# One of a block's three picked tiles is made inside the softmax, in spare columns of the sums' bank, and a block's first group has no pick

## The chip, the cores and the metric

The kernel runs on one core of one Trainium2 chip. The metric is device time in microseconds (us) of one execution. The engines named below are PE (TensorE, matrix multiply), DVE (VectorE), ACT (ScalarE), POOL (GpSimd) and SP (SyncE, which here only waits, loads registers and issues DMAs).

## The reference, cut to what matters

Four graph layers run one after another on a graph of N = 3125 nodes and E = 100000 edges, sorted by destination. The change touches only the second one, a GATv2 network with three attention layers. Each computes, for every edge, a logit from two node rows, a softmax over the edges that end in the same node, and a weighted sum:

```python
for Wl, bl, Wr, br, att, bo, g, be in layers:      # three layers
    h_new = gelu(layer_norm(gatv2(h, src, dst, n, Wl, bl, Wr, br, att, bo), g, be))
    h = h + h_new if h.shape == h_new.shape else h_new

def _gatv2(h, src, dst, n, Wl, bl, Wr, br, att, bias):
    xl = (h @ Wl + bl).reshape(n, H, C)            # 4 heads of 32
    xr = (h @ Wr + br).reshape(n, H, C)
    e = leaky_relu(xl[dst] + xr[src], 0.2)
    logit = einsum('ehc,hc->eh', e, att)
    ex = exp(logit - segment_max(logit, dst)[dst])
    alpha = ex / (segment_sum(ex, dst)[dst] + 1e-16)
    return segment_sum(alpha[..., None] * xr[src], dst).reshape(n, H * C) + bias
```

## The kernel before

`attention` (L614 on) is called three times. Edges are cut into 800 tiles of 125; four tiles are a *quad*, so there are 200 quads. Destination nodes are cut into 25 windows of 125. A *step* is a quad with one window that it touches: 224 steps. Sixteen steps are a *block* (14 blocks, numbered from 0), four steps a *group* (4 groups in a block, i = 0 to 3).

**Source rows.** A tile needs 125 rows of `xr`, picked by `src`. Most come by POOL, one indirect DMA a tile (L565), into a ring of 20 quads (`rows`). The fourth tile of every fifth quad (40 tiles in all, the *picks*) is made by PE instead: DVE writes a one-hot matrix `hot_n` of 3125 x 125 in three cuts of windows (`point`, L941 to L946, each a compare of the tile's source numbers, laid out in PSUM as `wide_srcs`, against the node numbers), PE multiplies it with `xr` in 25 matmuls, again in three cuts (`pick`, L860 to L866), into `mixture`, columns of the second bank of `turn`; ACT copies it out and stores it to memory (`store_picked`, L750 to L756), and SP fetches it into the ring when its quad comes up (`fetch`). Thus POOL issues 760 indirect DMAs an attention. Four picks are made ahead; then blocks 0 to 11 make three each, in their groups 0, 1 and 2; blocks 12 and 13 make none.

**Who lets POOL go on.** POOL works down the quads in order (`gather_quads`). Before quad x it waits on `kept` (L563), which SP raises (`free`, in `pass_quads`) when quad x - 20 has been weighed by DVE for the last time (`weighted`). SP also passes on to PE, by `here` (L590), that a quad has landed.

**A block's steps.** For step k of block b, PE spreads the destination rows and adds the source rows (`spread_rows`, L835 to L847, matmuls L843 and L846, one step ahead of DVE), DVE makes the logits (`logits`, L977, L981, L984). In the same turn DVE weighs the rows of step k - 16, the same step of the block before (`weigh`, L992), PE sums them (`sum_rows`, L857), and DVE adds the sums on (`add_team`, L1000). So rows stay in the ring from their logit until the block's softmax is done and a block later they are weighed. Block 0 weighs nothing (`alone` in DVE's code, `spreads` in PE's and ACT's).

**The softmax between two blocks.** PE transposes the logits (L873). DVE runs eight scans (L1010, L1011); PE transposes their ends (L877) and then the carries (L881); DVE shifts the logits by the maxima (L1032 to L1038); ACT exponentiates them (L760); PE loads the next four steps' numbers into registers (`step_places`) and transposes the weights back (L887) and makes one small matmul (L888); ACT makes `fade` (L762); DVE copies the weights to `tail` and fades the running sums (L1042 to L1051). Then the next block begins: ACT lays out the source numbers of its picks (`lay`, L748, it waits for the softmax's end, since these lie in the bank that the softmax uses), and DVE's first instruction is the first `point`, which waits for it.

The order of every engine's work is the order of the code; semaphores alone tie the engines together.

Of the kernel before, what the change touches and what calls it, by code (L numbers as in the profile page):

```python
# [15 lines left out]
E = 100000  # L16
# [37 lines left out]
LAST = (PICKS - FIRST) // PER  # L54
assert RING % PICK == 0 and FIRST <= GROUP and PER <= GROUP and E // RROWS == 2 * HALF * P and FIRST + PER * LAST == PICKS and LAST < BLOCKS - 1
GROUPS = (WIN + 3) // 4
# [364 lines left out]
def hold(eng, sem, value, held_up):  # L421


    eng.wait_ge(sem, value)
    eng.sem_inc(held_up, 1)
# [222 lines left out]
def attention(nc, g, table, xl, xr, ft, att, own_att, own_logit):  # L648
# [4 lines left out]
    with Scope(nc) as sc:  # L653
# [39 lines left out]
        held_up_too = sc.sem("held_up_too")  # L693
        srcs_in, laid, noded, mixed, evicted, stored, fetching, returned = (sc.sem(x) for x in ("srcs_in", "laid", "noded", "mixed", "evicted", "stored", "fetching", "returned"))
# [28 lines left out]
        def _(act):  # L723
# [25 lines left out]

            def store_picked(t):  # L750
# [3 lines left out]
                act.copy(picked, mixture).then_inc(evicted, 1)  # L754
# [25 lines left out]

            with act.Fori(0, PER) as i:
                spreads(i)
                store_picked(i + FIRST)
            if PER < GROUP:
                with act.Fori(PER, GROUP) as i:
                    spreads(i)
            for q in range(2):
                load_hot(q, q)
            weigh(0)

# [6 lines left out]

            def block_of(b, per):
                if per:
                    with act.Fori(0, per) as i:  # L800
                        group(b, i)
                        store_picked(PER * b + i + FIRST)
                if per < GROUP:
                    with act.Fori(per, GROUP) as i:
                        group(b, i)
                weigh(b)

            with act.Fori(1, LAST) as b:
                lay(b + 1)
                act.wait_ge(laid, b + 2)  # L810
                load_srcs(PER * b + PER + FIRST)
                block_of(b, PER)
            with act.Fori(LAST, BLOCKS) as b:
                block_of(b, 0)
            last = TEAMS - BSTEPS
# [15 lines left out]
        def _(pe):  # L831
# [27 lines left out]

            def pick(t, r):  # L860
                pe.wait_ge(noded, len(CUTS) * t + r + 1)
                if r == 0 and not (isinstance(t, int) and t == 0):
                    pe.wait_ge(evicted, t)
                for w in range(*CUTS[r]):
                    ins = pe.matmul(mixture, hot_n[:, w, :], xr[:, w, :], start=w == 0, stop=w == WIN - 1)  # L865
# [24 lines left out]

            def four_steps(b, i, places=None, picking=True):
                for q in range(AHEAD):
                    k = BSTEPS * b + AHEAD * i + q
                    if q or not (isinstance(i, int) and i == 0):
                        sum_rows(k - BSTEPS - 1, (q - 1) % AHEAD)
                    if places is None:
                        places = step_places(nc, pe, g, k + 1)
                    if picking and q:
                        pick(PER * b + i + FIRST, q - 1)
                    spread_rows(k + 1, GROUP * b + i + (q + 1) // AHEAD, (q + 1) % AHEAD, places[q])  # L900
# [7 lines left out]
            def spreads(i, picking):  # L908
                places = step_places(nc, pe, g, AHEAD * i + 1)
                for q in range(AHEAD):  # L910
                    if picking and q:
                        pick(i + FIRST, q - 1)
                    spread_rows(AHEAD * i + q + 1, i + (q + 1) // AHEAD, (q + 1) % AHEAD, places[q])

            with pe.Fori(0, PER) as i:
                spreads(i, True)
            if PER < GROUP:
                with pe.Fori(PER, GROUP) as i:
                    spreads(i, False)
            def block_of(b, per, picked_by):  # L920
                four_steps(b, 0, softmax(b - 1, picked_by=picked_by), per > 0)
                if per > 1:
                    with pe.Fori(1, per) as i:
                        four_steps(b, i)
                if per < GROUP:
                    with pe.Fori(max(per, 1), GROUP) as i:
                        four_steps(b, i, None, False)
                sum_rows(BSTEPS * b - 1, AHEAD - 1)

            with pe.Fori(1, LAST) as b:  # L930
                block_of(b, PER, PER * b + FIRST)
            with pe.Fori(LAST, BLOCKS) as b:
                block_of(b, 0, PICKS)
            softmax(BLOCKS - 1, more=False)
# [5 lines left out]
        def _(dve):  # L940
# [45 lines left out]
            def choose(b, i, q):  # L986
                if q < len(CUTS):
                    point(PER * b + i + FIRST, i, q)

# [64 lines left out]

            dve.wait_ge(laid, 2)

            def alone(i, picking):
# [5 lines left out]

            with dve.Fori(0, PER) as i:
                alone(i, True)
            if PER < GROUP:
                with dve.Fori(PER, GROUP) as i:
                    alone(i, False)
            softmax(0)
# [15 lines left out]

            def block_of(b, per):
                both(b, 0, per > 0)
                if per > 1:
                    with dve.Fori(1, per) as i:
                        both(b, i, True)  # L1090
                if per < GROUP:
                    with dve.Fori(max(per, 1), GROUP) as i:
                        both(b, i, False)
                ws = windows_of(nc, dve, g, BSTEPS * b - 2, 2)
# [4 lines left out]
            with dve.Fori(1, LAST) as b:  # L1099
                dve.wait_ge(laid, b + 2)  # L1100
                block_of(b, PER)
            with dve.Fori(LAST, BLOCKS) as b:
                block_of(b, 0)
            last = TEAMS - BSTEPS
# [1628 lines left out]
```

## Time and profile before

| | us |
|---|---|
| median of 3 runs | 6526.3 (6516.55 to 6531.65) |
| profiled execution, its own time | 6522.1 |
| profiled execution, span of its trace | 6520.3 |

Busy time is 4622.5 us on PE (71% of the span), 3864.3 us on DVE (59%), 3852.1 us on POOL (59%), 1597.9 us on ACT (25%). The three attentions take from about 1080 to 2300 us, 2388 to 3600 us and 3694 to 4920 us of the span. A timeline row reads: start in us, duration in us, engine, line, operation, output<-input, and in brackets the idle time before it with what ended it. "issue" means that nothing which the profile shows was waited for; an engine's name with q is its sequencer, so `SPq L577` is SP's raising of `kept`.

### The profile page before, as it was taken

Reading aid. Unit: us, or ns where it says so; the run is one execution under the profiler, and the core shown is the slowest. Engines: PE = TensorE matmul, PEld = TensorE weight load, DVE = VectorE, ACT = ScalarE, POOL = GpSimd, SP = SyncE. Lnnn points to the kernel's source line nnn. Section 1 sums busy time; section 2 is a strip of 40 time slices with the busy share of each in tenths; the row PEclk is TensorE's granted clock in tenths of the full one; section 3 lists DMA queues with packets and bytes.
Section 4 is the critical chain, followed back from the end, with each engine's and each line's share of the span. In section 5 each row is a group of like instructions: output and inputs, shape, how many; then the busy total and the mean of one; then the engine's idle time right before and its main releaser. Section 6 shows DMA issues by size and latency. Waiting matters only on the chain. (4 is left out here: it accounts for less than half of the span.)

```text
span 6520.3 us, 133948 instructions
## 1 busy us (share of the span) xinstructions
PE 4622.5 (71%) x34231; PEld 4074.0 (62%) x34232; DVE 3864.3 (59%) x9164; ACT 1597.9 (25%) x3365; POOL 3852.1 (59%) x3152
## 2 busy tenths in 40 slices
PE   7868874787888747888887477887763656666665
PEld 5765334677777646777776467777762455555554
DVE  8988126666666566666665766666656433333334
ACT  4764110111111111111111111111111144444443
POOL 0000002778787726887877268878780078888884
PEclk9989986898888878988887788888886778778777
DMA  6863441333333323333333233333331122222221
GB/s 160 221 167 117 121 121 49 80 98 98 98 99 97 96 68 80 98 99 99 99 96 96 68 79 98 99 98 97 93 99 43 47 66 66 65 65 65 66 65 46
DMA packets 633590, 600.24 MB, mean 92 GB/s; under 512 B 244880, under 2 KB 571807, under 8 KB 632685
## 3 DMA queue, kind: packets, MB, share of 16 engines
q0 software_dynamic: 250880, 233.27, 15.7%
q10 hardware_dynamic: 229475, 208.97, 11.0%
q1 hardware_dynamic: 153097, 156.30, 9.0%
q8 instruction: 71, 1.16, 0.1%
q14 instruction: 67, 0.54, 0.0%
HBM read 497.47 MB, written 97.37 MB: 91 GB/s over the span
## 5 line engine op out<-in xcount | busy, mean ns | idle before, releaser
L565 POOL DMA_INDIRECT rows<-row_table,now x2280 | 2829.2, 1241 | 1640.8 <-issue 1527.6
L565 POOL DMA_INDIRECT rows<-node_table,now x800 | 989.9, 1237 | 562.9 <-issue 562.9
L977 DVE SCALAR_TENSOR_TENSOR z<-zp,own 125x512 f32<-125x512 f32 x672 | 464.1, 691 | 832.7 <-PE zp L846 828.1
L857 PEld LDWEIGHTS sums<-both,hot 125*125 125x125 f32 x5376 | 773.9, 201 | 186.9 <-issue 125.8
L857 PE MATMUL sums<-both,hot 125*125 125x137 f32 x5376 | 808.7, 297 | 101.6 <-ACT both L739 73.9
L846 PE MATMUL zp<-rows,ident 125*125 x2700 | 819.2, 430 | 70.2 <-SPq L590 68.9
L865 PE MATMUL turn<-xr,ft 125*125 125x132 f32 x6000 | 785.9, 289 | 70.2 <-DVE ft L946 66.1
L843 PE MATMUL zp<-parts,hot_t 125*125 x8100 | 654.7, 234 | 242.3 <-issue 183.6
L865 PEld LDWEIGHTS turn<-xr,ft 125*125 125x125 f32 x6000 | 760.1, 200 | 76.6 <-DVE ft L946 68.9
L843 PEld LDWEIGHTS zp<-parts,hot_t 125*125 125x125 bf16 x8100 | 614.1, 145 | 278.7 <-issue 276.5
L738 ACT CAST hot<-hot 125x500 f32<-125x500 bf16 x672 | 408.7, 608 | 1479.9 <-PE sums L857 751.1
L846 PEld LDWEIGHTS zp<-rows,ident 125*125 125x125 f32 x2700 | 492.1, 203 | 135.6 <-issue 77.6
L1273 DVE TENSOR_TENSOR z<-zp,rows 125x512 f32<-125x512 f32 x224 | 155.0, 692 | 628.8 <-SPq L590 503.5
L1206 PE MATMUL turn<-ident,onehot 125*126 125x125 f32 x904 | 175.6, 328 | 484.6 <-issue 464.7
L992 DVE TENSOR_TENSOR both<-rows,xl 125x512 f32 (+1 forms) x672 | 462.3, 688 | 87.7 <-PE sums L857 81.6
L946 DVE TENSOR_TENSOR ft<-turn,nodes 125x1125 f32<-125x1125 f32 x360 | 447.4, 1244 | 95.7 <-ACT turn L748 46.3
L981 DVE TENSOR_REDUCE both<-z 125x16 f32<-125x512 f32 x672 | 456.6, 679 | 1.6
L1206 PEld LDWEIGHTS turn<-ident,onehot 125*126 125x126 f32 x904 | 115.5, 165 | 529.2 <-issue 507.0
L1223 PE MATMUL sums<-values,onehot 125*125 125x129 f32 x1792 | 331.4, 346 | 0.0
L1214 PE MATMUL zp<-pb,onehot_t 126*125 x1792 | 327.7, 343 | 2.8 <-issue 0.6
L1498 DVE TENSOR_SCALAR hot<-nodes,both 125x522 bf16<-125x522 f16 x896 | 315.6, 416 | 19.1 <-PE bank L1537 18.8
L1214 PEld LDWEIGHTS zp<-pb,onehot_t 126*125 126x125 f32 x1792 | 306.8, 257 | 10.6 <-issue 8.2
(454 smaller groups left out, 5575.7 us busy)
## 6 DMA issues: line engine op xcount, KB each, us to landing
hot<-hots ACTq DMA_DIRECT2D x896, 122.1 KB
hot_t<-hots_t ACTq DMA_DIRECT2D x678, 122.1 KB
counts<-pairs SPq DMA_DIRECT2D x55, 685.1 KB
rows<-row_table,now POOLq DMA_INDIRECT x2280, 3.6
spread_slots<-slot_table POOLq DMA_DIRECT2D x56, 488.3 KB, 5.5
hots_t<-hot_t SPq DMA_DIRECT2D x112, 218.8 KB
hots<-hot_dst SPq DMA_DIRECT2D x112, 218.8 KB
pairs<-cells SPq DMA_DIRECT2D x25, 685.1 KB
```

The source lines that it names most:

```text
L565: pool.indirect_dma_start(rows[:, q, j, :], None, table, bass.IndirectOffsetOnAxis(ap=now[:, n, lane + j:lane + j + 1], axis=0)).then_inc( ...
L738: act.copy(hot32[:, q % 2, :], hot[:, q, :]).then_inc(made, 1)
L843: pe.matmul(zp[:, p, j, 0:ROW], hot_t[:, q, j * P:(j + 1) * P], own[part], start=part == 0 and j % 2 == 0, stop=False, skip_group_check=True)
L846: ins = pe.matmul(zp[:, p, 2 * half:2 * half + 2, 0:ROW], g.ident[0:P, 0:P], rows[:, bass.ds(at, 1), 2 * half:2 * half + 2, :].rearrange(" ...
L857: ins = pe.matmul(sums[:, p, 0:ACCW], hot32[:, p, j * P:(j + 1) * P], values[:, p, j, :], start=j == 0, stop=j == HALF - 1)
L865: ins = pe.matmul(mixture, hot_n[:, w, :], xr[:, w, :], start=w == 0, stop=w == WIN - 1)
L946: dve.tensor_tensor(hot_n[:, lo:hi, :], src, each(nodes[:, lo:hi], P), ALU.is_equal).then_inc(noded, 1)
L977: dve.scalar_tensor_tensor(out=z[:, p, :, :], in0=zp[:, p, :, 0:D], scalar=0.0, in1=rows_of(own_att, HALF), op0=ALU.max, op1=ALU.mult).the ...
L981: dve.tensor_reduce(bent[:, p, :, :], z[:, p, :, :].rearrange("p j (h c) -> p j h c", h=HEADS), AX_X, ALU.add).then_inc(reduced, 1)
L992: dve.tensor_tensor(values[:, q % 2, :, 0:D].rearrange("p j (h c) -> p j h c", h=HEADS), rows[:, bass.ds(at, 1), :, 0:D].rearrange("p a j ...
L1214: ins = pe.matmul(zp[:, p, j, :], onehot_t[:, p, j * P:(j + 1) * P], own[:, bass.ds(w, 1), :].rearrange("p w f -> p (w f)"), start=True, s ...
L1223: ins = pe.matmul(sums[:, q % 2, 0:width], onehot[:, q, j, 0:P], values[:, q % 2, j, :], start=j == 0, stop=j == HALF - 1)
```

## The change

- A block makes its three picks differently spread: none in group 0, one each in groups 1 and 2, and the third (its one-hot cuts made by DVE in group 3) by PE within the softmax that ends the block: the first cut behind the transposes of the logits, the second and third behind the transposes of the carries.
- This third pick, the *late* one, goes to `late`, columns 256 to 387 of the second bank of `sums`; PE waits for the last `add_team` before it writes there (`accd`) and for ACT's copy (`evicted`) before it goes on to the next block.
- ACT stores it between its two exponentials of the softmax. `lay` moves behind ACT's group 0, and DVE waits for it behind its own group 0.
- PE's code of blocks 12 and 13 is written out, not looped.

```diff
+        late = sums[:, 1, 256:256 + ROW]
...
-            def weigh(b):
+            def weigh(b, picking):
                 act.wait_ge(shifted, b + 1)
                 act.activation(weight[:, :, :], weight[:, :, :], ACT.Exp).then_inc(exped, 1)
+                if picking:
+                    store_picked(PER * b + PER - 1 + FIRST, late)
                 act.wait_ge(weights_turned, b + 1)
                 act.activation(fade[:, :], sums[:, 0, 256:256 + HEADS], ACT.Exp).then_inc(faded, 1)
...
             with act.Fori(1, LAST) as b:
...
+                group(b, 0)
+                if IDLE == 0:
+                    store_picked(PER * b + FIRST)
+                else:
+                    lay_next(b)
+                with act.Fori(1, GROUP - 1) as i:
+                    group(b, i)
+                    store_picked(PER * b + i - IDLE + FIRST)
+                group(b, GROUP - 1)
+                weigh(b, True)
...
-            def softmax(b, more=True, picked_by=None):
+            def softmax(b, more=True, picked_by=None, late_pick=None):
                 if picked_by is not None:
                     hold(pe, evicted, picked_by, held_up_too)
+                if late_pick is not None:
+                    hold(pe, noded, len(CUTS) * (late_pick + 1), held_up_too)
                 hold(pe, summed, after(BSTEPS * b + BSTEPS - 1), held_up_too)
                 for h in range(HEADS):
                     ins = pe.transpose(turn[0:BT, 0, h * P:(h + 1) * P], logit[:, :, h], g.ident[0:P, 0:P])
                 ins.then_inc(turned, 1)
+                if late_pick is not None:
+                    hold(pe, accd, after(BSTEPS * b - 1), held_up_too)
+                    pick(late_pick, 0, late)
...
                 ins.then_inc(carry_turned, 1)
+                if late_pick is not None:
+                    for r in range(1, len(CUTS)):
+                        pick(late_pick, r, late)
                 places = step_places(nc, pe, g, BSTEPS * b + BSTEPS + 1) if more else None
                 hold(pe, exped, b + 1, held_up_too)
...
+                if late_pick is not None:
+                    hold(pe, evicted, late_pick + 1, held_up_too)
                 return places
...
+            with pe.Fori(1, LAST) as b:
+                four_steps(b, 0, softmax(b - 1, picked_by=PER * b + FIRST - 1, late_pick=PER * b + FIRST - 1), IDLE == 0)
+                with pe.Fori(1, GROUP - 1) as i:
+                    four_steps(b, i)
+                four_steps(b, GROUP - 1, None, False)
                 sum_rows(BSTEPS * b - 1, AHEAD - 1)
...
             with dve.Fori(1, LAST) as b:
-                dve.wait_ge(laid, b + 2)
-                block_of(b, PER)
+                if IDLE == 0:
+                    dve.wait_ge(laid, b + 2)
+                both(b, 0, IDLE == 0)
+                if IDLE:
+                    hold(dve, laid, b + 2, laid_seen)
+                rest_of(b, True)
```

**PE in the softmax.** Before (the softmax at the head of the loop over blocks 1 to 11; `both` is the buffer in which the logits lie):

```order
L873 MATMUL turn<-ident,both 64x125 x4
L877 MATMUL turn<-ident,ends 4x64 x2
L881 MATMUL turn<-ident,carry_t 64x4 x2
L615 ISA
L615 TENSOR_LOAD place
L887 MATMUL turn<-ident,xl 125x64 x8
L888 MATMUL sums<-delta,slot 125x4
```

and now:

```order
L885 MATMUL turn<-ident,both 64x125 x4
L425 REGISTER_ALU
L871 ISA
L875 MATMUL sums<-xr,ft 125x132 x9
L892 MATMUL turn<-ident,ends 4x64 x2
L896 MATMUL turn<-ident,carry_t 64x4 x2
L871 REGISTER_ALU
L875 MATMUL sums<-xr,ft 125x132 x8
L871 REGISTER_ALU
L875 MATMUL sums<-xr,ft 125x132 x8
L616 ISA
L616 TENSOR_LOAD place
```

Nine matmuls now stand between the transposes of the logits and of the ends, and sixteen between the transposes of the carries and the register load. [...]

**DVE at the start of a block.** Before (the end of the softmax, and the first instructions of the block; `ft` holds the one-hot matrix, `turn` the source numbers laid out by ACT):

```order
L1051 TENSOR_TENSOR acc<-acc,sums 125x4
L1099 UNCONDITIONAL_BRANCH
L1099 ISA
L944 ISA
L946 TENSOR_TENSOR ft<-turn,nodes 125x1125
L975 ISA
L976 REGISTER_ALU
L977 SCALAR_TENSOR_TENSOR z<-zp,own 125x512
L624 ISA
L624 TENSOR_LOAD pair
L991 REGISTER_ALU
```

and now:

```order
L1072 TENSOR_TENSOR acc<-acc,sums 125x4
L1112 UNCONDITIONAL_BRANCH
L1112 ISA
L997 REGISTER_ALU
L998 SCALAR_TENSOR_TENSOR z<-zp,own 125x512
L625 ISA
L625 TENSOR_LOAD pair
L1012 REGISTER_ALU
L1013 ISA
L1013 TENSOR_TENSOR both<-rows,xl 125x4x128
```

The compare is gone from between the softmax and the first logit, and with it the wait for ACT's `lay`.

**ACT around the softmax's end.** Before (`xl` is the buffer in which the weights lie):

```order
L760 ACTIVATE xl<-xl 64x500
L762 ACTIVATE fade<-sums 125x4
L808 UNCONDITIONAL_BRANCH
L808 ISA
L748 CAST turn<-srcs 125x375
```

and now:

```order
L762 ACTIVATE xl<-xl 64x500
L756 COPY both<-sums 125x132
L146 DMA picked_rows<-both 112x132
L146 DMA picked_rows<-both 13x132
L766 ACTIVATE fade<-sums 125x4
L808 UNCONDITIONAL_BRANCH
L808 ISA
```

A copy and two stores stand between the exponentials, and the layout of the source numbers no longer follows them.

## Rows read from the trace of the kernel before

**Rows 1.** The page's busy times of all engines: us, share of the span, instructions.

```profile
PE 4622.5 (71%) x34231; PEld 4074.0 (62%) x34232; DVE 3864.3 (59%) x9164; ACT 1597.9 (25%) x3365; POOL 3852.1 (59%) x3152
```

**Rows 2.** Engines' busy times (and counts) from 1220 to 2278 us, clock, DMA.

```profile
1220.00:2278.00 1058.00, 837.05 (x6769) 776.69 (x6768) 688.09 (x1565) 173.28 (x477) 845.17 (x683) 0.88 0.38 98
```

**Rows 3.** POOL's only group there: count | busy us, mean ns | idle before.

```profile
L565 POOL DMA_INDIRECT rows<-row_table,now x683 | 846.4, 1239 | 232.3 <-issue 197.6 <-SPq L577 34.8
```

**Rows 4.** POOL's timeline: one ordinary gather, then the ones behind a stall.

```profile
1309.37 1.21 POOL L565 DMA_INDIRECT rows<-row_table,now  x1 [0.30 <-issue]
...
1218.81 1.21 POOL L565 DMA_INDIRECT rows<-row_table,now  x1 [19.68 <-SPq L577]
...
3831.93 1.21 POOL L565 DMA_INDIRECT rows<-row_table,now  x1 [21.20 <-SPq L577]
...
1307.85 1.21 POOL L565 DMA_INDIRECT rows<-row_table,now  x1 [1.46 <-SPq L577]
...
3280.98 1.21 POOL L565 DMA_INDIRECT rows<-row_table,now  x1 [3.12 <-SPq L577]
...
4593.22 1.21 POOL L565 DMA_INDIRECT rows<-row_table,now  x1 [1.82 <-SPq L577]
```

**Rows 5.** DVE's timeline, block 0 of the first attention and the start of block 1.

```profile
1146.67 1.33 DVE L946 TENSOR_TENSOR ft<-turn,nodes 125x1125 f32<-125x1125 f32 x1 [0.37 <-DVE carry_t L971]
...
1161.14 0.68 DVE L977 SCALAR_TENSOR_TENSOR z<-zp,own 125x512 f32<-125x512 f32 x1
...
1189.85 0.69 DVE L977 SCALAR_TENSOR_TENSOR z<-zp,own 125x512 f32<-125x512 f32 x1 [1.59 <-PE zp L846]
...
1200.18 0.22 DVE L1006 CAST brk<-brk 64x126 f32<-64x126 bf16 x1
...
1214.35 0.15 DVE L1051 TENSOR_TENSOR acc<-acc,sums 125x4 f32 x1
1215.32 1.33 DVE L946 TENSOR_TENSOR ft<-turn,nodes 125x1125 f32<-125x1125 f32 x1 [0.81 <-ACT turn L748]
1216.57 0.68 DVE L977 SCALAR_TENSOR_TENSOR z<-zp,own 125x512 f32<-125x512 f32 x1
1217.17 0.68 DVE L992 TENSOR_TENSOR both<-rows,xl 125x512 f32<-125x512 f32 x1
```

**Rows 6.** PE's timeline of the same stretch: picks, spreads, a load's gap, the softmax.

```profile
1148.06 4.10 PE L865 MATMUL turn<-xr,ft 125*125 125x132 f32 x18 [13.80 <-DVE ft L946]
...
1157.06 1.96 PE L865 MATMUL turn<-xr,ft 125*125 125x132 f32 x16
...
1162.79 1.08 PE L843 MATMUL zp<-parts,hot_t 125*125 x12 [2.13 <-issue]
1163.71 1.10 PE L846 MATMUL zp<-rows,ident 125*125 x4
...
1204.31 0.27 PE L877 MATMUL turn<-ident,ends 64*4 64x64 f32 x2 [3.11 <-DVEq L1016]
1206.06 0.20 PE L881 MATMUL turn<-ident,carry_t 4*64 4x4 f32 x2 [1.48 <-DVEq L1027]
1210.83 1.91 PE L887 MATMUL turn<-ident,xl 64*125 64x64 f32 x8 [4.58 <-ACT xl L760]
...
1213.18 1.58 PE L843 MATMUL zp<-parts,hot_t 125*125 x12
1214.55 2.06 PE L846 MATMUL zp<-rows,ident 125*125 x4
```

**Rows 7.** PE's timeline, the last spread ahead of the softmax after block 1.

```profile
1281.40 2.05 PE L846 MATMUL zp<-rows,ident 125*125 x4 [2.43 <-SPq L590]
```

**Rows 8.** DVE's timeline, the first step of a group without a pick.

```profile
1354.95 0.69 DVE L977 SCALAR_TENSOR_TENSOR z<-zp,own 125x512 f32<-125x512 f32 x1 [2.26 <-PE zp L846]
1355.92 0.69 DVE L992 TENSOR_TENSOR both<-rows,xl 125x512 f32<-125x512 f32 x1 [0.28 <-issue]
```

**Rows 9.** ACT's timeline: the second exponential of the softmax after block 0.

```profile
1213.29 0.17 ACT L762 ACTIVATE fade<-sums 125x4 f32<-125x4 f32 x1 [2.60 <-PE sums L888]
```

More of the change, by code:

```diff
@@ L54 @@
 LAST = (PICKS - FIRST) // PER
-assert RING % PICK == 0 and FIRST <= GROUP and PER <= GROUP and E // RROWS == 2 * HALF * P and FIRST + PER * LAST == PICKS and LAST < BLOCKS - 1
+IDLE = GROUP - PER
+assert RING % PICK == 0 and FIRST <= GROUP and IDLE in (0, 1) and E // RROWS == 2 * HALF * P and FIRST + PER * LAST == PICKS and LAST < BLOCKS - 1
 GROUPS = (WIN + 3) // 4
@@ L753, in store_picked @@
                     act.wait_ge(stored, landed(t - 1, len(PIECES)))
-                act.copy(picked, mixture).then_inc(evicted, 1)
+                act.copy(picked, bank).then_inc(evicted, 1)
                 act.wait_ge(evicted, t + 1)
                 wide(act, store[bass.ds(t, 1), :, :].rearrange("a p f -> (a p) f"), picked, stored)
-            def weigh(b):
+            def weigh(b, picking):
                 act.wait_ge(shifted, b + 1)
                 act.activation(weight[:, :, :], weight[:, :, :], ACT.Exp).then_inc(exped, 1)
+                if picking:
+                    store_picked(PER * b + PER - 1 + FIRST, late)
                 act.wait_ge(weights_turned, b + 1)
@@ L779, in spreads @@
                     load_spread(AHEAD * i + q + 2, (q + 2) % AHEAD)
-            with act.Fori(0, PER) as i:
+            spreads(0)
+            if IDLE == 0:
+                store_picked(FIRST)
+            with act.Fori(1, GROUP - 1) as i:
                 spreads(i)
[L783 to L786, printed above, removed]
+                store_picked(i - IDLE + FIRST)
+            spreads(GROUP - 1)
             for q in range(2):
                 load_hot(q, q)
-            weigh(0)
+            weigh(0, True)
             def group(b, i):
@@ L796, in group, with lay_next @@
                     load_hot(c + 2, (q + 2) % AHEAD)
[L798 to L808, printed above, removed]
+            def lay_next(b):
                 lay(b + 1)
@@ L811, in _ @@
                 load_srcs(PER * b + PER + FIRST)
-                block_of(b, PER)
+            with act.Fori(1, LAST) as b:
+                if IDLE == 0:
+                    lay_next(b)
+                group(b, 0)
+                if IDLE == 0:
+                    store_picked(PER * b + FIRST)
+                else:
+                    lay_next(b)
+                with act.Fori(1, GROUP - 1) as i:
+                    group(b, i)
+                    store_picked(PER * b + i - IDLE + FIRST)
+                group(b, GROUP - 1)
+                weigh(b, True)
             with act.Fori(LAST, BLOCKS) as b:
-                block_of(b, 0)
+                with act.Fori(0, GROUP) as i:
+                    group(b, i)
+                weigh(b, False)
             last = TEAMS - BSTEPS
@@ L858, in sum_rows, with pick @@
                 ins.then_inc(closed, 1)
-            def pick(t, r):
+            def pick(t, r, bank=mixture):
                 pe.wait_ge(noded, len(CUTS) * t + r + 1)
@@ L898, in four_steps @@
                     if picking and q:
-                        pick(PER * b + i + FIRST, q - 1)
+                        pick(PER * b + i - IDLE + FIRST, q - 1)
                     spread_rows(k + 1, GROUP * b + i + (q + 1) // AHEAD, (q + 1) % AHEAD, places[q])
@@ L911, in spreads @@
                     if picking and q:
-                        pick(i + FIRST, q - 1)
+                        pick(i - IDLE + FIRST, q - 1)
                     spread_rows(AHEAD * i + q + 1, i + (q + 1) // AHEAD, (q + 1) % AHEAD, places[q])
-            with pe.Fori(0, PER) as i:
+            spreads(0, IDLE == 0)
+            with pe.Fori(1, GROUP - 1) as i:
                 spreads(i, True)
[L917 to L927, printed above, removed]
-                sum_rows(BSTEPS * b - 1, AHEAD - 1)
[L930 to L933, printed above, removed]
+            spreads(GROUP - 1, False)
+            with pe.Fori(1, LAST) as b:
+                four_steps(b, 0, softmax(b - 1, picked_by=PER * b + FIRST - 1, late_pick=PER * b + FIRST - 1), IDLE == 0)
+                with pe.Fori(1, GROUP - 1) as i:
+                    four_steps(b, i)
+                four_steps(b, GROUP - 1, None, False)
+                sum_rows(BSTEPS * b - 1, AHEAD - 1)
+            for b in range(LAST, BLOCKS):
+                if b == LAST:
+                    places = softmax(b - 1, picked_by=PICKS - 1, late_pick=PICKS - 1)
+                else:
+                    places = softmax(b - 1, picked_by=PICKS)
+                four_steps(b, 0, places, False)
+                with pe.Fori(1, GROUP) as i:
+                    four_steps(b, i, None, False)
+                sum_rows(BSTEPS * b - 1, AHEAD - 1)
             softmax(BLOCKS - 1, more=False)
@@ L987, in choose @@
                 if q < len(CUTS):
-                    point(PER * b + i + FIRST, i, q)
+                    point(PER * b + i - IDLE + FIRST, i - IDLE, q)
             def weigh(c, i, q, at):
@@ L1053, in softmax @@
                 assert s.n == SOFT, s.n
-            dve.wait_ge(laid, 2)
             def alone(i, picking):
@@ L1062, in alone @@
                         pass
-            with dve.Fori(0, PER) as i:
+            dve.wait_ge(laid, 2)
+            alone(0, IDLE == 0)
+            with dve.Fori(1, GROUP) as i:
                 alone(i, True)
-            if PER < GROUP:
-                with dve.Fori(PER, GROUP) as i:
-                    alone(i, False)
             softmax(0)
@@ L1084, in both, with rest_of @@
                             add_team(c - 2, (q - 2) % AHEAD, pairs[q][1])
[L1086 to L1093, printed above, removed]
+            def rest_of(b, picking):
+                with dve.Fori(1, GROUP) as i:
+                    both(b, i, picking)
                 ws = windows_of(nc, dve, g, BSTEPS * b - 2, 2)
```

11 lines of the change are left out of this document (6 added, 5 removed).

## The prediction

> **What bounds the kernel now.** I read the busy times of the page first, then those of one attention, then POOL's waits and timeline, and last the stretch around block 0 on DVE and PE. Over the whole span PE is busiest, 71% against POOL's 59% [rows 1]. Within an attention they are level: of 1058 us from 1220 to 2278 us PE is busy 837 us and POOL 845 us [rows 2]. So the gaps have to tell. POOL's only group there has 683 gathers of 1.239 us; the idle time before them is 232.3 us, 197.6 us of it "issue" and 34.8 us a wait for SP [rows 3]. The ordinary gap is 0.30 us, and a gather comes 1.51 us after the one before [rows 4]. That gap is POOL's own turn-around: it stands before gathers that waited for nothing. Of the 34.8 us, 19.4 us belong to the gather at 1218.81 us, 35 ordinary gaps make 10.5 us, and 4.8 us are left. From 1220 us to the last gather POOL thus stands still for 4.8 us of 1058. The other engines make 25 matmuls more or less beside it; the attention ends a fixed tail after POOL's last gather.
>
> A change that adds or removes no gather can only win what POOL loses in stalls. There are two kinds [rows 4]. The first: the ring is full, and POOL waits until block 1 begins to weigh: 19.68, 21.75 and 21.20 us in the three attentions, less the ordinary 0.30 each: 61.7 us (the second lies between the two shown). The second: nine short stalls behind softmaxes, the first of 1.46 us at 1307.85 us, the longest of 3.12 us at 3280.98 us, the last of 1.82 us at 4593.22 us; less the ordinary gaps 12.9 us in sum. Together 75 us: no gain can be above that while POOL is the bound.
>
> The short stalls have a pattern. By the reference's edge list the boundaries behind blocks 5 and 9 are those where 16 steps advance by 15 new quads, not 14, and behind block 1 the first quad to be released needs a second step. Six of the nine stalls, 10.7 us, stand behind blocks 5 and 9; one behind block 1; two of about 0.5 us behind block 4.
>
> **Block 0, part by part (first stall).** The stall ends 1.6 us after block 1's first weighing, at 1217.17 us [rows 4, 5]. So I ask how much earlier that comes.
>
> Group 0 loses its pick. It lasted from 1146.67 us to the first z of group 1 at 1161.14 us, 14.5 us, the compare of group 1 (1.25 us) within [rows 5]. A group without a pick is seen in group 3: 10.3 us, from 1189.85 to 1200.18 us [rows 5]. It holds the 2.13 us in which PE loads registers [rows 6], which in group 0 is done long before: 8.2 us. PE comes out of a long idle stretch, so its first spread takes 3.4 us (1213.18 to 1216.61 us, the lower clock) and not 2.0 us (1162.79 to 1164.81 us) [rows 6]: 9.6 us. With the compare 10.8 us, against 14.5 us: 3.7 us earlier. Followed step by step with the same durations it is 4.7 us, since group 3 had waits of its own. I take 4.2 us; bounds 2 and 5.
>
> Groups 1 and 2 keep their picks: 0. Group 3 gains three compares on DVE, one while it waits for PE anyway (1.59 us [rows 5]), the others in part within its later waits for PE: 0.3 us later; bounds 0 and 2.5 (two whole compares).
>
> The softmax gains 25 matmuls on PE. The first nine (18 in the trace) take 2.2 us by 1.96 us for 16 [rows 6], 4.1 us at the lower clock; the gap before the next transposes is 3.11 us [rows 6]. DVE's scans hide them at the higher clock; at the lower they cost 1 us. The sixteen others take 3.9 us or, at the lower clock, 4.10 x 32 / 18 = 7.3 us; behind them PE still loads registers, 2.13 us [rows 6], or 1.3 us if its sequencer is ahead of the matmuls (my estimate); the gap there is 4.58 us [rows 6]. So the transposes back start 0.6 to 1.4 us late at the higher clock and up to 4.8 us late at the lower. Queued behind them are the weights' transposes, ACT's fade, DVE's copies and the first weighing: all on the path. Against that, these transposes now take 1.91 us after idling [rows 6]; straight behind matmuls I expect about half, 0.9 us less. Value: 0.6 us later; bounds -0.9 and 4.8.
>
> The rows on the clock: a stretch right behind idle runs at half the pace (18 matmuls in 4.10 us, 16 in 1.96 us [rows 6]), that is 1.2 and 2.4 GHz. The Trainium skill, TensorE: Matmul & The Clock Gate, Part 1, says the same in reverse: throttled is the default, and activity releases it. By that rule the picks in the softmax pay for part of themselves; taken wholly, my 0.6 us would be 0.
>
> ACT's copy and its two stores stand before the fade. The fade waited 2.60 us for PE [rows 9]; the copy and the issue of two stores need less, so 0. PE's new waits (`accd`, `evicted`) end before PE gets there, since DVE adds the last team before the scans and ACT copies while PE transposes: 0, at worst 0.3 us.
>
> The start of block 1: from the softmax's last instruction (1214.35 us) to the first z (1216.57 us) 2.2 us pass, with the wait for `lay` and a compare [rows 5]; without them z follows at once, 2.0 us earlier. But the compare covered a register load on DVE: where there is none, the weighing starts 0.97 us behind z, not 0.60 us [rows 8, 5]. Net 1.6 us earlier; bounds 1 and 2.2. The layout itself moves behind ACT's first group and DVE meets it a whole group later: 0.
>
> First stall: 4.2 - 0.3 - 0.6 + 1.6 = 4.9 us shorter, three times: 14.7 us. The ends: -3.6 (longer) and +8 an attention.
>
> **Later blocks (short stalls).** Each loses a pick of some 6 us of PE time from its groups; compute reaches the softmax sooner, but PE then waits for the next quad to land, as at 1281.40 us, 2.43 us [rows 7]. From there POOL has room for a fixed number of gathers, so what counts is the time from the softmax to the first weighing, 1.0 us shorter (1.6 - 0.6). The nine stalls would lose 1.0 us each where nothing else moved: about 8 us gone. But four of the six behind blocks 5 and 9 were met with compute late, not waiting; caught up, each may grow by 1 us. I take 5 us won; bounds 12.9 won and, with a softmax 4.8 us longer, 28 us lost. The picks arrive later than before, but the quad that needs one comes up more than half a block later: 0. The tail behind the last gather and all other layers: 0.
>
> **Sum.** 14.7 + 5 = 19.7, say 20 us. Against the execution's own 6522.1 us (span 6520.3 us) this gives 6502 us; the median of the runs is 4.2 us above that execution, and the prediction is for the median: 6526.3 - 20 = 6506 us.
>
> **Rivals.** (A) Half swallowed: the sixteen matmuls fall for part of their time into the lower clock, because PE idles 3.11 and 1.48 us just before [rows 6]. With 2.5 us added instead of 0.6 the first stalls give 3 x 3.0 = 9 us and the short ones lose about 5: 4 us faster, 6522 us; between this and the forecast lies 6515 us. For it: the clock falls easily here, as the 1.91 us show. Against: the first nine matmuls now fill most of the first gap.
>
> (B) The softmax becomes longer than its cover, the other side. Place: between the carries' transposes and the weights' transposes in all 36 softmaxes with a pick. Price at the lower clock throughout: 4.8 us. Then first stalls gain 0.7 us each, the six boundaries behind blocks 5 and 9 stall 3.2 us more each, blocks 1 and 4 begin to: about 28 us lost, 26 us net, 6552 us. By these terms it decides from about 3.1 us of added softmax on. Against it: once sixteen matmuls run back to back the clock rises within them, as it does behind the 4.10 us pick [rows 6].
>
> (C) PE is the bound, and what leaves the groups is won: some 6.1 us a pick (2.2 + 1.96 + 1.96 [rows 6]) in 36 blocks, 220 us, 6306 us. For it speaks only that PE is busiest over the span [rows 1]. Against it are POOL's gaps [rows 3, 4]. The Trainium skill, Perfetto Trace Analysis, Identifying the Most-Contended Engine, names the engine of the highest occupancy; over the span that is PE, and by it this rival would be the forecast. In the stage itself the two differ by 1% [rows 2], too little to go by.
>
> (D) Nothing moves: block 0's gain is given back by something unseen, such as PE's longer code. 6526 us.
>
> **Chances.** Forecast 0.65, its own range 6494 to 6513 us; A 0.17; B 0.08; C 0.02; D 0.08. A difference of 0.2%, 13 us, is about what a measurement of this kernel tells from none. Faster by more: the forecast and C, and a little of A: 0.69. Within it: 0.24, A and D. Slower: 0.07, most of B. The range, 6493 to 6523 us, takes in the forecast, A and most of the bounds of block 0, and leaves out B and C.
>
> **What would show it.** In the new trace: as many gathers, 1.51 us apart; the three first stalls near 15 us each; the first weighing of block 1 about 65 us after DVE begins block 0 (now 70.5 us, 1146.67 to 1217.17 us [rows 5]); the transposes back under 1.5 us long; waits of PE for SP ahead of most softmaxes; short stalls only behind blocks 5 and 9. I am wrong if POOL shows gaps over 3 us there, if the first stalls stay above 18 us, or if an attention shortens by more than its stalls.

## The result, and the profile after

| | before, us | changed, us |
|---|---|---|
| median of 4 runs each | 6522.5 (6516.6 to 6531.7) | 6486.7 (6482.0 to 6493.7) |
| profiled execution, span | 6520.3 | 6485.3 |

The ratio is 0.9943 with a 95% interval of 0.9931 to 0.9955: 29 to 45 us faster, 36 us by the medians. The forecast was 20 us, 6506 us, with a range that ended at 6493 us. Of the 19 us between 6506 and 6487 us, 4 us are the starting point: the forecast counted from 6526.3 us, and a fourth run has moved the median before to 6522.5 us. The direction came true and POOL's stalls went as the mechanism says; the size was wrong, and part of the gain came from something that the forecast had no term for.

The changed kernel's page, busy times (to be read against [rows 1]):

```profile
PE 4652.9 (72%) x34231; PEld 4079.2 (63%) x34232; DVE 3860.7 (60%) x9164; ACT 1596.1 (25%) x3365; POOL 3843.4 (59%) x3152
```

Its engines from 1215 to 2266 us (clock and DMA at the end; [rows 2]), and POOL's group there ([rows 3]):

```profile
1215.00:2266.00 1051.00, 846.64 (x6779) 777.65 (x6779) 689.90 (x1567) 172.87 (x478) 842.16 (x683) 0.92 0.39 98
```

```profile
L566 POOL DMA_INDIRECT rows<-row_table,now x683 | 842.5, 1234 | 225.4 <-issue 191.7 <-SPq L578 33.7
```

The same 683 gathers take 1051 us instead of 1058 us. The granted clock is 0.92 on average, not 0.88: PE has nearly the same work, part of it now in a stretch in which it idled. POOL's timeline, each attention's first stall and the two longest short ones ([rows 4]):

```profile
1214.63 1.21 POOL L566 DMA_INDIRECT rows<-row_table,now  x1 [16.88 <-SPq L578]
...
2507.31 1.21 POOL L566 DMA_INDIRECT rows<-row_table,now  x1 [11.70 <-SPq L578]
...
3802.34 1.21 POOL L566 DMA_INDIRECT rows<-row_table,now  x1 [14.18 <-SPq L578]
...
1965.40 1.21 POOL L566 DMA_INDIRECT rows<-row_table,now  x1 [0.96 <-SPq L578]
...
4217.44 1.21 POOL L566 DMA_INDIRECT rows<-row_table,now  x1 [0.96 <-SPq L578]
```

The first stalls fell from 61.8 us to 41.9 us in sum (less the ordinary 0.30 us each), the short ones from 12.9 us to 1.8 us. PE in the softmax behind block 0 ([rows 6]; the trace has two records for each matmul of a pick, so nine read x18 and sixteen x32):

```profile
1198.59 0.59 PE L885 MATMUL turn<-ident,both 125*64 125x125 f32 x4
1199.02 2.26 PE L875 MATMUL sums<-xr,ft 125*125 125x132 f32 x18
1202.29 0.27 PE L892 MATMUL turn<-ident,ends 64*4 64x64 f32 x2 [1.02 <-DVEq L1037]
1204.03 0.19 PE L896 MATMUL turn<-ident,carry_t 4*64 4x4 f32 x2 [1.47 <-DVEq L1048]
1204.17 3.86 PE L875 MATMUL sums<-xr,ft 125*125 125x132 f32 x32
1209.05 1.05 PE L905 MATMUL turn<-ident,xl 64*125 64x64 f32 x8 [1.02 <-ACT xl L762]
```

The first part of the pick fits its gap, and the transposes behind the second take 1.05 us instead of 1.91 us, at a granted clock of 1.00 instead of 0.50. The second part does not always fit. What the transposes back need is ACT's exponential; here it is before, here behind block 0 of the changed kernel, and behind its block 1 with PE beside it:

```profile
1210.07 0.62 ACT L760 ACTIVATE xl<-xl 64x500 f32<-64x500 f32 x1 [13.33 <-DVEq L1039]
```

```profile
1208.04 0.62 ACT L762 ACTIVATE xl<-xl 64x500 f32<-64x500 f32 x1 [13.87 <-DVEq L1060]
...
1287.95 0.62 ACT L762 ACTIVATE xl<-xl 64x500 f32<-64x500 f32 x1 [18.35 <-DVEq L1060]
...
1289.56 1.05 PE L905 MATMUL turn<-ident,xl 64*125 64x64 f32 x8 [0.28 <-issue]
```

Before, the transposes start 0.14 us after the exponential's end (1210.69 to 1210.83 us [rows 6]), and so in all 36 softmaxes. In the changed kernel they start 0.39 us after it behind block 0, although the row names ACT as the releaser, and 0.99 us after it behind block 1. In 22 of its 36 softmaxes with a pick it is more than 0.3 us; the mean of the 36 is 0.67 us. So the pick, with the register load behind it, makes the transposes back some 0.5 us late.

DVE at the start of block 1 ([rows 5]):

```profile
1211.52 0.15 DVE L1072 TENSOR_TENSOR acc<-acc,sums 125x4 f32 x1
1211.99 0.69 DVE L998 SCALAR_TENSOR_TENSOR z<-zp,own 125x512 f32<-125x512 f32 x1 [0.32 <-DVE acc L1072]
1212.98 0.69 DVE L1013 TENSOR_TENSOR both<-rows,xl 125x512 f32<-125x512 f32 x1 [0.30 <-issue]
```

From the end of the softmax to the first weighing 1.46 us pass instead of 2.82 us. And PE now waits for gathers far oftener: the page's groups of the last spread matmul, before and after (idle time at the end of the row):

```profile
L846 PE MATMUL zp<-rows,ident 125*125 x2700 | 819.2, 430 | 70.2 <-SPq L590 68.9
```

```profile
L856 PE MATMUL zp<-rows,ident 125*125 x2700 | 841.4, 439 | 192.2 <-SPq L591 191.2
```

PE's waiting for `here` grew from 69 us to 191 us: most of what compute won went into waiting for the gathers.

### The profile page after: what moved, and what is told of

It reads as the page before. It is cut to its first block and busy times, and to the rows that moved or that the text cites. A ratio compares the mean times of both kernels' runs of the same rounds, so it can differ in the third digit from the quotient of the medians.

```text
span 6485.3 us, 133849 instructions
## 1 busy us (share of the span) xinstructions
PE 4652.9 (72%) x34231; PEld 4079.2 (63%) x34232; DVE 3860.7 (60%) x9164; ACT 1596.1 (25%) x3365; POOL 3843.4 (59%) x3152
## 3 DMA queue, kind: packets, MB, share of 16 engines
q10 hardware_dynamic: 229475, 208.97, 11.1%
## 5 line engine op out<-in xcount | busy, mean ns | idle before, releaser
L856 PE MATMUL zp<-rows,ident 125*125 x2700 | 841.4, 439 | 192.2 <-SPq L591 191.2
L867 PEld LDWEIGHTS sums<-both,hot 125*125 125x125 f32 x5376 | 799.8, 206 | 194.2 <-issue 121.2
L867 PE MATMUL sums<-both,hot 125*125 125x137 f32 x5376 | 825.2, 300 | 113.0 <-ACT both L741 75.5
L875 PE MATMUL turn<-xr,ft 125*125 125x132 f32 x4200 | 521.9, 280 | 28.1 <-DVE ft L967 24.0
L875 PEld LDWEIGHTS turn<-xr,ft 125*125 125x125 f32 x4200 | 504.7, 192 | 32.1 <-DVE ft L967 24.7
```

Of the source, the lines that this page charges most:

```text
L856: ins = pe.matmul(zp[:, p, 2 * half:2 * half + 2, 0:ROW], g.ident[0:P, 0:P], rows[:, bass.ds(at, 1), 2 * half:2 * half + 2, :].rearrange(" ...
L867: ins = pe.matmul(sums[:, p, 0:ACCW], hot32[:, p, j * P:(j + 1) * P], values[:, p, j, :], start=j == 0, stop=j == HALF - 1)
L875: ins = pe.matmul(bank, hot_n[:, w, :], xr[:, w, :], start=w == 0, stop=w == WIN - 1)
```

## The experiments

Each is timed against the kernel before on its own chip. "Gathers" is the sum over 2280 gathers of their duration above 1.21 us. "Softmax" runs from the start of DVE's first softmax instruction to the start of its last, "start" from there to the first weighing, means over blocks 1 to 11.

| kernel | ratio to before (95%) | first stalls, us | short stalls, us | gathers, us | softmax, us | start, us |
|---|---|---|---|---|---|---|
| before | | 61.8 | 12.9 | 73.6 | 14.34 | 2.91 |
| before again | 1.0004 (0.9993 to 1.0014) | 61.8 | 14.3 | 70.0 | 14.34 | 2.91 |
| changed | 0.9943 (0.9931 to 0.9955) | 41.9 | 1.8 | 62.9 | 13.68 | 1.74 |
| changed again | 0.9943 (0.9929 to 0.9956) | 41.8 | 0 | 64.2 | 13.69 | 1.74 |
| shift only | 0.998 (0.997 to 0.999) | 61.0 | 13.2 | 61.9 | 14.47 | 1.74 |
| softmax only | 0.9979 (0.997 to 0.9989) | 49.2 | 9.8 | 75.3 | 13.52 | 2.94 |
| late pick of 3 matmuls | 0.9956 (0.9942 to 0.9969) | 45.4 | 6.4 | 64.3 | 14.29 | 1.75 |
| late pick doubled | 1.0013 (1.0003 to 1.0023) | 58.8 | 27.6 | 69.2 | 17.82 | 1.73 |
| before, 600 gathers | 0.9793 (0.9775 to 0.9811) | | | | | |
| changed, 600 gathers | 0.952 (0.9504 to 0.9536) | | | | | |
| work deferred, changed | 0.9905 (0.9891 to 0.992) | 12.7 | 1.5 | 67.7 | 13.65 | 1.78 |
| work deferred, before | 0.9945 (0.9933 to 0.9957) | 21.8 | 17.6 | 75.6 | 14.39 | 2.92 |

**The changed kernel and the kernel before, once more.** Both kernels run again as they are.

> The changed kernel as it is, to see again what its profile shows. Theory S (stalls): POOL's gathers bound each attention, and the change wins what POOL's stalls lose: about 20 us of the three first stalls and 11 us of the short ones. Then this run again has first stalls of 11 to 17 us and nearly no short ones, and is 30 to 40 us faster than before. The sum of the gathers' durations above 1.21 us was 74 us before and 63 us in the changed kernel's profile. If that is the change's doing (theory G, gathers got cheaper), it comes out at 60 to 66 us again; if it is chance, anywhere from 60 to 75 us. Rival P (PE is the bound, and 36 picks out of the groups are won) would want over 200 us faster and is already out.

> The kernel before as it is, for a second profile of it. So far the gathers' durations above 1.21 us sum to 74 us in the kernel before and 75 us with the softmax half alone (both lay out the source numbers at the block's start and pick in group 0), and to 61 to 64 us in the four profiles whose group 0 is free. Theory G (the arrangement does it) expects 70 to 78 us here, theory chance anything from 60 to 78 us. First stalls of 19 to 22 us and short ones of 8 to 15 us in sum are expected again.

Measured 6485.2 us and 6519.3 us. Stalls and softmax repeat closely; the gathers' durations repeat to 1.3 and 3.6 us. In this pair of profiles they differ by 5.8 us, not by 10.7 us as in the first.

**The placement alone.** Group 0 has no pick, and the third one stays in the old bank, in group 3 (PE's part of the edit):

```diff
-                four_steps(b, 0, softmax(b - 1, picked_by=PER * b + FIRST - 1, late_pick=PER * b + FIRST - 1), IDLE == 0)
-                with pe.Fori(1, GROUP - 1) as i:
-                    four_steps(b, i)
-                four_steps(b, GROUP - 1, None, False)
+                four_steps(b, 0, softmax(b - 1, picked_by=PER * b + FIRST), IDLE == 0)
+                with pe.Fori(1, GROUP) as i:
+                    four_steps(b, i)
```

> The changed kernel, but the third pick is made by PE in group 3, in the old bank, not in the softmax; group 0 has no pick and the layout comes behind ACT's group 0, as in the changed kernel. Theory S: block 0 has as many picks on PE as before, so it is as long as before, and only the block's start is shorter (1.6 us): first stalls 1 to 2 us shorter than before each, short stalls 1 us each, together 8 to 15 us faster than before. Rival R: the free first group is what counts (it lets compute run ahead right behind the softmax), then nearly the whole 35 us are here.

Measured 6509.7 us, 13 us faster by the ratio (7 to 20): theory S's figure, but not its items, so the hit is luck. The stalls hardly moved (61.8 to 61.0, 12.9 to 13.2 us); the gathers got 11.7 us cheaper. For the first stalls the trace shows why: block 1 starts 1.4 us sooner behind its softmax, but with a pick right ahead of it the softmax behind block 0 takes 15.3 us instead of 14.1 us, since PE begins its first transposes 1.2 us later. R, that the free first group is what counts, falls.

**The softmax pick alone.** Groups 0 and 1 pick, the third pick is made in the softmax, and the layout stays at the block's start (the constant and PE's part of the edit):

```diff
-IDLE = GROUP - PER
+IDLE = 0
...
-                with pe.Fori(1, GROUP - 1) as i:
-                    four_steps(b, i)
-                four_steps(b, GROUP - 1, None, False)
+                four_steps(b, 1)
+                with pe.Fori(2, GROUP) as i:
+                    four_steps(b, i, None, False)
```

> The other half alone: the third pick is made in the softmax, but groups 0 and 1 hold the other two, the one-hot cuts of the third are written in group 2, and the layout stands at the block's start as before. Theory S: block 0 is shorter by the pick that left it, about 4 us, the softmax is as in the changed kernel, the block's start is as before: first stalls 4 us shorter than before each, short stalls half gone, together 17 to 25 us faster than before. Rival R: 0 to 8 us faster.

Measured 6509.7 us, 14 us faster by the ratio, less than the 17 to 25 us expected. The first stalls lose 12.6 us (4.2 each, as expected), the short ones 3.1 us, not the expected half, the gathers lose nothing. The halves give 27 us by their ratios, the whole 37 us; the intervals leave it open whether that gap is real. The profiles point the same way: the short stalls lose 3.1 us and nothing in the halves and 11 us or more in the whole. That they need both the shorter softmax and the shorter start is my reading, not shown by a run of its own.

**Fewer matmuls in the late pick.** Twenty-two of its 25 matmuls are left out, so the picked rows are wrong:

```diff
-                for w in range(*CUTS[r]):
+                some = range(*CUTS[r]) if bank is mixture else range(CUTS[r][0], CUTS[r][0] + 1)
+                for w in some:
...
```

> The changed kernel with 3 of the late pick's 25 matmuls (one in each cut; the other 22 are left out, so the picked rows are wrong). It prices what the matmuls cost in the softmax. If they are covered (theory S as measured: the softmax got 0.7 us shorter beyond the block's start), the time is within 6 us of the changed kernel, and the transposes back may even be slower, since PE idles and its clock falls again: 1.9 us instead of 1.0 us. If they cost 1 us or more in each softmax, this kernel is 3 us faster by the first stalls and up to 5 us by what is left of the short ones.

Measured 6493.9 us (6489.0 to 6496.0), against 6485.2 us (6478.9 to 6489.8) for the changed kernel on the same chip: 8.7 us slower, a little past the 6 us of "covered". The stalls are 8 to 10 us longer than in the two profiles of the changed kernel. The softmax with 22 matmuls less on PE is 0.6 us longer. Its PE timeline:

```profile
1203.09 1.24 PE L876 MATMUL sums<-xr,ft 125*125 125x132 f32 x4
1207.75 1.91 PE L906 MATMUL turn<-ident,xl 64*125 64x64 f32 x8 [3.41 <-ACT xl L762]
1209.58 0.58 PE L907 MATMUL sums<-delta,slot 1*125 1x4 f32 x2
```

PE idles 3.41 us and then takes 1.91 us for the transposes, at a granted clock of 0.50; behind the full pick it takes 1.05 us at 1.00. The transposes here start 0.15 us after the exponential's end in every softmax, against 0.67 us in the mean with the full pick. So the 22 matmuls cost 0.5 us in front of the transposes and give back more behind them, by the higher clock: they are more than free.

**The late pick doubled.** Its 25 matmuls are done twice, so the picked rows come out doubled:

```diff
+                times = 1 if bank is mixture else 2
+                for n in range(times):
+                    for w in range(*CUTS[r]):
+                        ins = pe.matmul(bank, hot_n[:, w, :], xr[:, w, :], start=w == 0 and n == 0, stop=w == WIN - 1 and n == times - 1)
```

> The changed kernel with the late pick's 25 matmuls done twice (so its rows come out wrong by the doubled sums). At the higher clock they then take 4.5 us in the first gap of 3.1 us and 7.7 us in the second of 4.6 us: the softmax becomes 3 to 5 us longer. Theory S: first stalls 3 to 5 us longer each, the boundaries behind blocks 5 and 9 stall again by 2 to 4 us each: 20 to 40 us slower than the changed kernel. If the softmax is not on the path that sets POOL's stalls, under 8 us.

Measured 6528.4 us, 43 us (medians) to 46 us (ratios) slower than the changed kernel, a little past the 20 to 40 us expected, and 8 us slower than before. PE in the softmax behind block 0, and one of POOL's longest short stalls:

```profile
1195.47 4.29 PE L877 MATMUL sums<-xr,ft 125*125 125x132 f32 x36
1199.68 0.27 PE L894 MATMUL turn<-ident,ends 64*4 64x64 f32 x2
1201.20 0.19 PE L898 MATMUL turn<-ident,carry_t 4*64 4x4 f32 x2 [1.25 <-DVEq L1050]
1201.33 7.46 PE L877 MATMUL sums<-xr,ft 125*125 125x132 f32 x64
1209.78 1.05 PE L907 MATMUL turn<-ident,xl 64*125 64x64 f32 x8 [0.99 <-issue]
```

```profile
1977.89 1.21 POOL L566 DMA_INDIRECT rows<-row_table,now  x1 [5.55 <-SPq L578]
```

The softmax is 4.1 us longer, the first stalls grow by 5.6 us each, and the short ones come back at 27.6 us. This is rival B of the prediction, made to happen. The first part now ends past its gap (the transposes of the ends follow it without a wait), and the transposes back start 3.6 us after the exponential's end: the second gap, which the single pick already overran in 22 of 36 softmaxes, is left far behind.

**Only 600 gathers an attention, before and changed.** POOL fetches three tiles of every quad; the fourth tile's rows are left out, so the output is wrong:

```diff
-            for j in range(HALF - 1 if by_engine(q, picks) else HALF):
+            for j in range(HALF - 1 if picks else HALF):
```

> The kernel before with three gathers by POOL for every quad, not four for four quads out of five (the fourth tile's rows are left out, so the output is wrong): 600 gathers an attention, whose 1.55 us make some 930 us. It takes the bound away from POOL and shows what compute alone needs. Theory S: compute needs about as long as the gathers did (a block 82 us), so an attention is 1120 to 1190 us between the same marks and the time 0 to 200 us less than before. Theory P (PE bounds already) expects the same time as before within 20 us.

> The changed kernel with the same 600 gathers. Theory S: with POOL's bound gone the change is worth what compute wins in a block, 5 to 7 us in each of 36 blocks, so this is 150 to 250 us faster than the kernel before with 600 gathers. If the two differ by less than 60 us, compute did not win much in the blocks and my account of where the gain is hidden is wrong.

Measured 6382.6 us, 138 us less than before, and 6208.4 us: with POOL out of the way the change is worth 174 us, against 36 us with it. A block of blocks 1 to 11 takes 82.0 us in the kernel before and 77.3 us in the changed one (mean distance of DVE's first softmax instructions), 4.7 us less. POOL's group from 1300 to 2100 us in the changed kernel with 600 gathers:

```profile
L566 POOL DMA_INDIRECT rows<-row_table,now x444 | 556.3, 1253 | 243.6 <-issue 238.1 <-SPq L578 5.5
```

444 gathers in 800 us, where [rows 3] has 683 in 1058 us: POOL waits now. The profile books this as "issue" too, but 444 ordinary gaps of 0.30 us are 133 us of the 238.1 us, and single gaps are 9 us and more behind softmaxes. Rival C's bound was wrong for this kernel; its price, 6.1 us a pick, was 1.4 us above the 4.7 us that a block wins.

**The first stall attacked directly.** DVE's work ahead of block 0 that nothing needs before block 1 is taken out there and goes between block 0's logits (the place where it goes in):

```diff
                     for _ in logits(AHEAD * i + q, i, q):
                         pass
+                    for _ in range(2 if i == 0 or q == AHEAD - 1 else 1):
+                        if rest_of_start:
+                            rest_of_start.pop(0)()
```

> The changed kernel, with DVE's work that no one needs before block 1 (the nodes' own logits, 20 instructions of 0.82 us, and the clearing of the sums, 3.1 us) taken out of the stretch ahead of block 0 and put between the logits of block 0, where DVE waits for PE for some 15 us. Nothing is left out. Theory S: what an attention takes is POOL's gathers plus its stalls, and the first stall (11 to 17 us) is the largest left. Block 0 starts 20 us earlier and lasts 6 to 10 us longer, so the first weighing comes 10 to 14 us earlier and the first stall shrinks to 1 to 5 us: 30 to 42 us faster than the changed kernel. If the stall is not what the time hangs on, less than 15 us.

> The same move in the kernel before (picks in groups 0 to 2). Its block 0 has the same idle time on DVE (about 15 us), its first stalls are 20 to 22 us. Theory S: first stalls 8 to 12 us, short ones as before, 30 to 42 us faster than before; so the change and this move add up.

Measured 6450.2 us and 6477.9 us. The changed kernel with the move is 0.9905 of the kernel before, less than with either edit alone. Its POOL timeline around the first stall:

```profile
1199.66 1.21 POOL L566 DMA_INDIRECT rows<-row_table,now  x1 [0.30 <-issue]
1206.12 1.21 POOL L566 DMA_INDIRECT rows<-row_table,now  x1 [5.25 <-SPq L578]
```

First stalls of 4.95, 3.80 and 3.92 us are left (less 0.30 us), 29 us less than in the changed kernel; the time fell by 25 us by the ratios and 35 us by the medians, which were taken on different chips. On the kernel before, the move takes 40 us from the first stalls, a little more than expected (6.2 to 8.0 us each are left, not 8 to 12), and 36 us (ratio) to 39 us (medians) from the time. The two edits add up nearly: 62 us together by the ratio, 73 us as a sum of the two.

## Why the prediction was wrong

The steps that failed are the sum's term for the short stalls, the sign of its softmax term, and the gathers' own cost, which it took as fixed. The stalls fell as the mechanism says, but more than forecast (31.0 us in the first pair of profiles, 34.4 us in the second, not 19.7 us), and the gathers themselves, for which the sum had no term, got cheaper by 10.7 and 5.8 us. One of the prediction's own signs of being wrong came true: the attentions shortened by more than their stalls, by 41.6 us in the first pair.

**Right: what bounds the kernel.** POOL's gathers bound an attention. Doubling the pick (43 to 46 us), deferring work (36 to 39 us in the kernel before) and freeing POOL (138 us, and 174 us between the two kernels then) each moved the time the way this says. But what the prediction drew from it, that only POOL's stalls can be won, was wrong.

**Right: block 0.** Forecast 4.2 - 0.3 = 3.9 us shorter. From DVE's last clearing to its first softmax instruction: 54.1, 57.8 and 55.5 us before, 52.9, 49.2 and 52.4 us in the changed kernel, 4.3 us less in the mean (4.2 us between the two repeats). The single attentions gained 1.2, 8.6 and 3.1 us, so that the mean came out within 0.4 us is partly luck.

**Wrong by its sign: the softmax.** The term was 0.6 us *longer*; measured 0.5 to 0.6 us *shorter* behind block 0 (14.12 to 13.62 us in the first pair, 14.16 to 13.54 us in the second) and 0.66 us in blocks 1 to 11. Both halves of the term were about right. Late start of the transposes back: forecast 0.6 to 1.4 us at the higher clock, measured 0.53 us in the mean over 36 softmaxes. Their own time: forecast 0.9 us less, measured 0.86 us less. These two alone make -0.3 to +0.5 us; the 0.6 us put down lies above both and leaned towards the lower clock, which hardly came: the mean granted clock over the late pick's matmuls is 0.91. Two gains were not in the term: the small matmul ends 0.31 us behind the transposes instead of 0.51 us, and the exponential ends 0.13 us sooner. The run with three matmuls shows that the gain comes from the matmuls. The rule of the Trainium skill, TensorE: Matmul & The Clock Gate, Part 1, that activity releases the throttle, agrees with this trace (1.91 us at a granted clock of 0.50, 1.05 us at 1.00).

**Slightly off: the block's start.** Forecast 1.6 us shorter, measured 1.4 us behind block 0 and 1.2 us later.

**The first stalls** came out 6.6 us shorter each instead of 4.9 us: 19.9 us instead of 14.7 us. The softmax's sign makes 1.1 us of the 1.7 us.

**Wrong in size: the short stalls.** Forecast 5 us of 12.9 us won, measured 11.1 us (14.3 us in the second pair). I had taken 1.0 us off each and given four of six back, as compute that has caught up would meet the ring later. What came off was 1.8 us each (0.66 + 1.17), and nothing was given back. The experiments lay the short stalls against softmax plus start: 27.6 us of stalls at 19.6 us, 12.9 and 14.3 at 17.3, 9.8 at 16.5, 13.2 at 16.2, 6.4 at 16.0, 1.8 and 0 at 15.4. More time goes with more stalls, at some 6 to 7 us for 1 us between 17.3 and 15.4 us, about one for each of the six boundaries behind blocks 5 and 9. But the placement alone (13.2 at 16.2) won nothing where 1 us came off, so softmax plus start is not all that sets them; what else does stays open.

**Missing: the gathers' own durations.** The prediction put the gathers at a fixed cost and the sum had no term for them. They fell by 10.7 us in the first pair of profiles and by 5.8 us in the second. The four profiles with a pick in group 0 show 73.6, 70.0, 75.3 and 75.6 us, the six without 62.9, 64.2, 61.9, 64.3, 69.2 and 67.7 us: 8.6 us between the means, no overlap, though the nearest two are 0.8 us apart. The two kernels with 600 gathers differ the same way (89 us before, 68 us changed, over 1800 gathers). So the arrangement has a part in it; how, stays open. In the kernel before, 184 of the 232 gathers over 1.25 us overlap a weighing (L992, two operands from SBUF), of the other 2048 only 566. That suggests DVE and POOL in each other's way, but it is a coincidence counted: all 184 also overlap the reduction and the addition behind the weighing (L981, L984), and no run was made that changes one of them alone.

The account of the first pair: first stalls -19.9 us, short stalls -11.1 us, gathers' durations -10.7 us, together -41.7 us between the first and last gathers; +6.7 us outside them (4.4 us of it behind the last attention, where the code is the same), -35.0 us in all. The second pair: -20.1, -14.3 and -5.8 us, with +3.2 us outside. What lies outside I take for scatter; no run shows it.

Two slips in the prediction's sums: the lower end of a first stall's gain is -4.3 us by its own bounds (2 - 2.5 - 4.8 + 1), not -3.6 us, and its upper ends (3 x 8 + 12.9 us) reach past the 6493 us at which the range stopped, to 6489 us.

Rivals A and B did not happen, B only when forced; C's bound is refuted, and D, no change, is outside the measured interval.

## What to carry to other kernels

Where two engines are equally busy, look at the gaps of each: the one with nothing but its ordinary turn-around between its instructions is the bound, and an edit elsewhere is worth that engine's stalls, plus what its own instructions get cheaper (here 6 to 11 us of some 40). Then list those stalls and price the edit on the path that ends each of them, here the time from a softmax to the first weighing. Work put on PE within a gap can shorten what follows it, so the price of such a move has a sign to be decided from the rows at both clock levels. And a row names one releaser: whether the moved work was late is told by the time from the awaited end to the start, over all repeats, here 0.14 us before and 0.67 us after.

## What the runs showed of the hardware that I had not expected

- Twenty-two matmuls more in each of 36 idle stretches made the whole kernel 8.7 us faster (6493.9 to 6485.2 us), with eight transposes behind them at 1.05 us instead of 1.91 us, though these started 0.5 us later.
- The duration of an indirect DMA on POOL is not fixed: most take 1.21 us, about a tenth 1.25 to 1.73 us, and the sum above 1.21 us differed between the arrangements (62 to 76 us over 2280).
- A second writer's columns in the bank that PE and DVE use for the sums cost nothing that the profile shows: PE's wait for DVE's last addition is 10 us over 36 softmaxes, within a gap that was idle before, and the transposes behind that gap start 3.49 us into the softmax, 3.53 us before.
